# Another order of the projections over the heads of a fused attention and feed-forward kernel, and a constant copy in four parts

## The reference

```python
xn = layernorm(x)
q, k, v = xn @ Wq + bq, xn @ Wk + bk, xn @ Wv + bv          # 16 heads of 32 columns
scores = q @ k.T / sqrt(32) + slope[head] * distance         # causal
attn_out = softmax(scores) @ v @ Wo + bo
gate_w, up_w, down_w = cubic interpolation of control points # 2048 x 512, 2048 x 512, 512 x 2048
ffn_out = (silu(xn @ gate_w.T) * (xn @ up_w.T)) @ down_w.T
out = x + attn_out + ffn_out                                
```

## Time and profile before

| | us |
|---|---|
| median of three runs | 837.47 (837.46 to 837.83) |
| the profiled execution | 838.84 |
| its span from first to last instruction | 837.0 |
| attention, first scores to the start of feed-forward | 37.97 to 524.87 |
| TensorE busy | 711.5 (85%) |
| VectorE busy | 507.2 (61%) |
| ScalarE busy | 439.3 (52%) |
| GpSimd busy | 332.3 (40%) |
| mean granted TensorE clock | 0.922 |

### The profile page before, as it was taken

How to read it: one execution, slowest core, us unless ns; L and a number is a source line. 1 busy time by engine, 2 the same in 40 slices (tenths; PEclk the granted TensorE clock), 3 DMA queues, 4 the chain that set the end, 5 groups by cost and what they waited for, 6 DMA issues and landing times. The chain is left out here.

```text
span 837.0 us, 14001 instructions
## 1 busy us (share of the span) xinstructions
PE 711.5 (85%) x4884; PEld 563.2 (67%) x4884; DVE 507.2 (61%) x1289; ACT 439.3 (52%) x961; POOL 332.3 (40%) x191
## 2 busy tenths in 40 slices
PE   5678779889789888898898676677978999999997
PEld 4556557667677776676676565455766888888886
DVE  6286687798979888967888688556432222222212
ACT  4266576687657766756877672334332333233321
POOL 2343453444534545534544450112214325425434
PEclk9878789899979999898999799679898999999999
DMA  7982654553584346465437945756616646433201
GB/s 254 188 219 37 111 74 155 76 76 65 114 182 101 48 76 114 93 173 77 67 68 210 252 143 170 245 153 187 208 51 196 224 118 202 153 108 105 101 1 50
DMA packets 53023, 109.78 MB, mean 131 GB/s; under 512 B 6361, under 2 KB 6617, under 8 KB 51417
## 3 DMA queue, kind: packets, MB, share of 16 engines
q1 hardware_dynamic: 51368, 106.46, 51.2%
q10 hardware_dynamic: 1584, 2.43, 1.2%
HBM read 59.32 MB, written 25.17 MB: 101 GB/s over the span
## 5 line engine op out<-in xcount | busy, mean ns | idle before, releaser
L1132 POOL TENSOR_TENSOR work<-work 128x1280 f16<-128x1280 f32 x64 | 168.4, 2632 | 235.2 <-DVE work L816 234.9
L1029 ACT ACTIVATE work<-work,neg_max 128x128 f32<-128x128 f32 (+3 forms) x256 | 142.3, 564 | 106.7 <-DVE neg_max L808 105.9
L1581 POOL TENSOR_TENSOR in_lo<-inner,in_hi 128x512 fp32r<-128x512 f32 x64 | 85.3, 1335 | 221.8 <-ACT in_hi L1497 221.8
L808 DVE CUSTOM_DVE_ANT_0 work<-bank,dist 128x128 f32<-128x128 f32 (+3 forms) x256 | 115.3, 487 | 89.0 <-PE bank L600 70.7
L1544 DVE TENSOR_TENSOR inner<-bank,silu 128x512 f32<-128x512 f32 x64 | 44.1, 689 | 136.0 <-ACT silu L1491 125.1
L1038 ACT COPY work<-bank 128x768 f16<-128x768 f16 (+1 forms) x128 | 110.0, 909 | 30.7 <-PE bank L614 29.5
L600 PE MATMUL bank<-k_stack,q_stack 96*128 96x256 f32 (+2 forms) x256 | 81.4, 396 | 45.2 <-issue 25.5
L1497 ACT CAST in_hi<-inner 128x512 fp32r<-128x512 f32 x64 | 39.7, 621 | 151.2 <-PE bank L1441 144.3
L614 PE MATMUL bank<-ident,work 128*128 128x128 f16 x1280 | 109.5, 230 | 10.2 <-DVE work L823 8.0
L614 PEld LDWEIGHTS bank<-ident,work 128*128 128x128 f16 x1280 | 78.4, 104 | 50.8 <-issue 35.2
L1439 PE MATMUL bank<-w_room,in_hi 128*128 128x512 f32 x256 | 102.7, 401 | 0.5 <-POOL in_lo L1581 0.5
(11 more groups left out here) (100 smaller groups left out, 1411.8 us busy)
## 6 DMA issues: line engine op xcount, KB each, us to landing
q_stack<-parts SPq DMA_DIRECT2D x48, 256.0 KB, 5.6
k_stack<-parts SPq DMA_DIRECT2D x48, 256.0 KB, 5.7
z<-xt_scratch SPq DMA_DIRECT2D x128, 88.0 KB
x_in<-x SPq DMA_DIRECT2D x32, 256.0 KB, 5.5
xt_scratch<-xt_room SPq DMA_DIRECT2D x8, 1024.0 KB, 6.8
xt_room<-xt_scratch SPq DMA_DIRECT2D x6, 1024.0 KB, 11.0
factor<-c_basis SPq DMA_DIRECT2D x5, 1024.0 KB, 7.9
taps<-windows SPq DMA_DIRECT2D x5, 1024.0 KB, 9.8
```

Source lines behind the costliest of these rows:

```text
L808: dve.tensor_tensor_reduce(probs[:, s % 2, OFF[i]:OFF[i] + n], score_bank[i % 2][:, 0:n], dist[:, S - n:S], -slope(s), 3.4e38, ALU.add, AL ...
L1029: e = act.activation(tile, tile, ACT.Exp, bias=neg_max[:, s % 2, i:i + 1], scale=-1.0, accum_out=row_sum[:, s % 4, i:i + 1])
L1132: pool.tensor_tensor(probs16[:, s % 2, 1, :], probs[:, s % 2, :], probs16[:, s % 2, 0, :], ALU.subtract).then_inc(lo_ready, 1)
L1581: pool.tensor_tensor(in_lo[k % 2][:, :], inner[:, k % 2, :], in_hi[:, k % 2, :].bitcast(F32), ALU.subtract).then_inc(il_ready, 1)
```

## The change

The order of units over the steps changes. Key tile 2 is projected at step 3 and not 5, key tile 3 at 8 (was 9), key tile 0 of the next batch at 12 (was 13), key tile 1 at 0 (was 1). q 1 moves to step 13 of the batch before, q 2 to step 1, q 3 to 7, q 0 to 11. The output tiles o 0 to o 3 are at steps 2, 4, 5 and 6 (were 2, 3, 6 and 7), v 1 is at step 13 (was 11). Steps 11 and 13 have two units, 9 and 10 none. Ahead of step 0 of batch 0 come now also v 3 and q 1. On VectorE, o 3 is added in step 7 after the first two maxima. `lay_out` is issued in four parts of 32 rows each between the other DMAs of batch 1's list, and sum 1 is stored behind `stack(b, 2)`.

```diff
--- before.py
+++ after.py
@@ -293,7 +293,7 @@
         in_lo = [room("in_lo0", [P, S], F32R, 78), room("in_lo1", [P, S], F32R, 40)]
 
         def load_basis(sp):
-            sp.wait_ge(bases_st, 16)
+            sp.wait_ge(bases_st, 64)
             sp.dma_start(bm_early[:].bitcast(F32).rearrange("p k e n -> p (k e n)"), moment_d).then_inc(bme_ld, 16)
             sp.dma_start(factor[2][:], c_factor[2]).then_inc(chunk_ld[2], 16)
 
@@ -366,8 +366,11 @@
                     tiles = each[:, m, 4 * (c - 1):4 * c, :].rearrange("p g n -> p (g n)")
                     eng.dma_start(tiles[other].bitcast(F32), tiles[own].bitcast(F32)).then_inc(dup_ld[c], 16)
 
-        def lay_out(sp):
-            sp.dma_start(bases_d, c_bases[:, 0:BM_COLS + BD_COLS]).then_inc(bases_st, 16)
+        def lay_out(sp, part):
+            rows = slice(part * P // 4, (part + 1) * P // 4)
+            sp.dma_start(bases_d[rows], c_bases[rows, 0:BM_COLS + BD_COLS]).then_inc(bases_st, 16)
+            if part:
+                return
             pad = xt_d[:, D:XT_ROWS, :].rearrange("a r n -> a (r n)").rearrange("a (k n) -> a k n", k=P // (2 * B))
             sp.dma_start(pad, c_zero.rearrange("(a k) n -> a k n", a=2 * B)).then_inc(pad_st, 16)
 
@@ -383,9 +386,9 @@
 
 HALF = H // 2
 
-UNITS = {0: [("q", 1)], 1: [("k", 1)], 2: [("o", 0)], 3: [("o", 1)], 4: [("q", 2)], 5: [("k", 2)], 6: [("o", 2)],
-         7: [("o", 3)], 8: [("q", 3)], 9: [("k", 3)], 11: [("v", 0), ("v", 1)], 12: [("q", 0)],
-         13: [("k", 0)], 14: [("v", 2)], 15: [("v", 3)]}
+UNITS = {0: [("k", 1)], 1: [("q", 2)], 2: [("o", 0)], 3: [("k", 2)], 4: [("o", 1)], 5: [("o", 2)], 6: [("o", 3)],
+         7: [("q", 3)], 8: [("k", 3)], 11: [("v", 0), ("q", 0)], 12: [("k", 0)], 13: [("v", 1), ("q", 1)],
+         14: [("v", 2)], 15: [("v", 3)]}
 TURNS = {2: [("c", 3)], 7: [("c", 0)], 9: [("x", 0), ("x", 1)], 10: [("x", 2), ("x", 3)], 11: [("c", 1)],
          15: [("c", 2)]}
 
@@ -404,7 +407,7 @@
     kind, n = key
     if s < HALF:
         return -1 if kind == "o" or key == ("c", 3) else 0
-    return 1 if kind in "xv" or (kind in "qk" and n == 0) else 0
+    return 1 if kind in "xv" or (kind in "qk" and n < 2) else 0
 
 
 def steps_keys(steps, before=True):
@@ -415,8 +418,8 @@
 STACK = 16 * ROLES
 
 
-PJ_FIRST = [("x", t) for t in range(QT)] + [("q", 0), ("k", 0), ("v", 0), ("v", 1), ("v", 2), ("q", 1), ("v", 3),
-                                            ("k", 1)] + steps_keys(range(2, HALF), before=False)
+PJ_FIRST = [("x", t) for t in range(QT)] + [("q", 0), ("k", 0)] + [("v", t) for t in range(QT)] + [("q", 1)] + (
+    steps_keys(range(HALF), before=False))
 PJ_BODY = steps_keys([*range(HALF, H), *range(HALF)])
 
 PJ_BODY_ENDS = list(PJ_BODY)
@@ -424,10 +427,10 @@
 PJ_BODY_ENDS.insert(PJ_BODY_ENDS.index(("c", 3)) + 1, ("o", 0))
 
 MOMENTS = {12: 0, 13: 1, 14: 2}
-PJ_LAST = [("q", 3), ("k", 3), ("c", 1), ("m", 0), ("m", 1), ("m", 2), ("c", 2), ("o", 0), ("o", 1), ("c", 3), ("o", 2), ("o", 3)]
-PJ_LAST_ENDS = [("q", 3), ("k", 3), ("c", 1), ("m", 0), ("m", 1), ("m", 2), ("c", 2), ("c", 3)] + [("o", t) for t in range(QT)]
-
-CARRIED = [("q", 3), ("k", 3)] + [("c", c) for c in range(1, KC)] + [("o", t) for t in range(QT)] + [
+PJ_LAST = [("k", 3), ("c", 1), ("m", 0), ("m", 1), ("m", 2), ("c", 2), ("o", 0), ("o", 1), ("c", 3), ("o", 2), ("o", 3)]
+PJ_LAST_ENDS = [("k", 3), ("c", 1), ("m", 0), ("m", 1), ("m", 2), ("c", 2), ("c", 3)] + [("o", t) for t in range(QT)]
+
+CARRIED = [("k", 3)] + [("c", c) for c in range(1, KC)] + [("o", t) for t in range(QT)] + [
     ("m", m) for m in range(3)]
 
 
@@ -724,12 +727,11 @@
                 turn_x(0, t)
             project_qk(0, "q", 0)
             project_qk(0, "k", 0)
-            for t in range(3):
+            for t in range(QT):
                 project_v(0, t)
+            project_qk(0, "q", 1)
             for s in range(HALF):
                 step(0, s, False)
-                if s == 0:
-                    project_v(0, 3)
             for b in range(1, B):
                 for s in range(HALF, H):
                     step(b - 1, s, True)
@@ -871,8 +873,6 @@
                         v_take(of, n)
                     elif kind == "o" and n > 0:
                         add_residual(of, n)
-                if not later(b) and s in (0, 1):
-                    v_take(b, s + 2)
                 if halved:
                     probs_high(*halved)
                 if s < H:
@@ -898,8 +898,6 @@
                     (x_low if kind == "x" else ctx_low)(of, n)
                 if carry and s == 3:
                     add_residual(b - 1, 0)
-                if carry and s == HALF - 1:
-                    add_residual(b - 1, QT - 1)
                 if carry and s in (8, 9):
                     norm_stats(b + 1, (2 * s - 16, 2 * s - 15))
                 for half, t in SPLITS.get(s, []):
@@ -943,7 +941,7 @@
             dve.tensor_tensor(parts[:, 1, :], qk_full[:], parts[:, 0, :].bitcast(F32), ALU.subtract
                               ).then_inc(ql_ready, 1)
             dve.wait_ge(dist_ld, 16)
-            for t in range(2):
+            for t in range(QT):
                 v_take(0, t)
             dve.wait_ge(wl_pool, 4)
             dve.wait_ge(wl_ready, 4)
@@ -1092,6 +1090,7 @@
             w_high(7)
             for t in range(2):
                 v_high(0, 0, t)
+            qk_high(0, "q", 1)
             for s in range(HALF):
                 step(0, s, False)
             for b in range(1, B):
@@ -1156,6 +1155,7 @@
                 pool.wait_ge(wh_ready, n + 1)
                 pool.tensor_tensor(w_piece(w_lo, n), w_raw[:, n % 3], w_piece(w_hi, n).bitcast(F32),
                                    ALU.subtract).then_inc(wl_pool, 1)
+            qk_low(0, "q", 1)
             for s in range(HALF):
                 step(0, s, False, False)
             for b in range(1, B):
@@ -1224,26 +1224,31 @@
                 load_piece(n)
             stack(0, 0)
             store_xt(0)
-
-            lay_out(sp)
             stack(0, 1)
             stack(0, 2)
             for b in range(1, B):
                 for t in range(QT):
                     load_x(b, t)
                 stack(b - 1, 3)
+                if b == 1:
+                    lay_out(sp, 0)
                 for q in range(QT):
                     sp.wait_ge(pj_full, pj_total(("x", q), b))
                     sp.nop(nofuse=True)
                     load_residual(b - 1, q)
                 store_xt(b)
                 stack(b, 0)
+                if b == 1:
+                    lay_out(sp, 1)
                 stack(b, 1)
+                if b == 1:
+                    lay_out(sp, 2)
                 store_sum(b - 1, 0)
-                store_sum(b - 1, 1)
                 stack(b, 2)
-                store_sum(b - 1, 2)
-                store_sum(b - 1, 3)
+                if b == 1:
+                    lay_out(sp, 3)
+                for q in range(1, QT):
+                    store_sum(b - 1, q)
                 for q in range(QT):
                     sp.wait_ge(res_st[q], 16 * b)
                 sp.nop(nofuse=True)
```

## The result

The changed kernel takes 800.84 us, median of 4 runs (796.64 to 803.49), against 837.47; the ratio is 0.9558, 95% interval 0.9511 to 0.9606. The forecast was 812, so the sign was right and the gain, 36.6 us, was 10.6 us larger than the 26.0 forecast; the time lies 1.2 us under the range.

A forecast was written before the change was run, and what follows sets the result against it. Attention was taken as TensorE-bound except for waits before scores, low-clock steps after them, and VectorE-bound steps 9 and 10. 14.3 + 10.4 + 8.4 + 3.4 - 10.5 = 26.0 us off 837.47 gave 812, range 802 to 823.

The forecast's parts named there:

- The six waits: TensorE's waits before scores at steps 0 and 8 of batches 1 to 3 go whole: 14.3 us less.
- The clock: Four steps (8 or 0) at the lower clock after a wait return to the upper one: 10.4 us less.
- The start: Steps 0 to 7 of batch 0 take 49.5 us, 8.4 less; v3 and q1 ahead of step 0 are hidden.
- The last batch: Step 12 of batch 3 comes 5.6 us earlier, 3.4 of it not yet counted; part of its wait stays.
- so k3 is bound by the queue: Last batch: q3 and k3 copies lie in the DMA queue behind residual loads, moment constants and the 1 MB factor.
- What it adds: Costs in steps 8 to 11 and 13 of batches 0 to 2: 3.5 us a batch, 10.5 in all.
- The +1.0 for q3's L1127 in step 8: POOL's low part of q3 meets VectorE's L839, which bounds through step 10: 1.0 us more a batch.
- The wait for x_low in step 11: Second unit there, q0, needs all x columns and waits for x_low: 0.6 us more a batch.
- rival (b): Clock falls earlier in step 9, stays low through 11, about 3 us a batch: 817 to 825, chance 0.18.
- Rival (c): Another engine, VectorE in steps 5 to 7 or ACT, takes over once waits go: 823 us, chance 0.12.
- Rival (d): Batch 0 reaches VectorE's bound of 44 and the end's queue has room, 10 us more gained: 802, chance 0.09.
- Rival (e): Idle time before L600 is the sequencer's own at these code places, so waits stay: 844 us, chance 0.03.

The follow-up runs named there:

- k0_early: Kernel before with q0 and k0 one step earlier each (11 and 12) and v1 two steps later (13): 828.28 us, ratio 0.9881.
- lay_whole: Changed kernel with the constants copied in one piece at their old place, behind the first store of xt: 805.60 us, ratio 0.9636.
- v3_late: Changed kernel with v3 and its v_take back behind the scores of step 0 of batch 0: 805.73 us, ratio 0.9604.
- q1_at_0: Changed kernel with q1 back beside k1 in step 0 of every batch and one unit in step 13: 819.61 us, ratio 0.9803.
- k2_early: Kernel before with q2 at step 3, k2 at 4, o1 at 5, and sum 1 stored behind the c = 2 stacks: 824.55 us, ratio 0.9849.
- k3_at_9: Changed kernel with q3 back in step 8, k3 in step 9, and no unit in step 7: 811.84 us, ratio 0.9693.
- low_first: Kernel before with a key's low part (L1127) ahead of probs_low (L1132) on POOL: 836.50 us, ratio 0.9986.

## Why the prediction was right in sign and too small

The six waits: the mechanism was right, and all nine but one went. **The step that failed is the price: "So the six at steps 0 and 8 of batches 1 to 3 go whole: 25.5 - 2.94 - 2.89 - 5.41 = 14.3 us".** They measured 18.4. I took the idle rows for the cost of the waits. Each wait cost 0.7 us more than its row in the mean, and step 15 before and in k0_early shows of what: 0.24 in how the record's end is modelled, and 0.5 because the late key's L1127 met VectorE's L793 (1.50 instead of 0.41 us). I had costed that kind of meeting in steps 8 and 10, and not in the steps 7 and 15 that these waits end.

The clock: 10.3 for 10.4, shown by the step windows, and by k0_early alone for steps 0 (5.61 us in all three batches, where two had taken 8.5).

The start: -10.5 for -8.4, with 1.1 given back by a later start. Step 4 began 25.5 us after step 0 (I had 25.8). Steps 4 to 7 took 21.90 where I had 22.19 + 1.4, since VectorE itself was busy for less there (21.10, from 22.19), and POOL too (11.77, from 13.01). The 1.1 us is in the load ahead of attention, where the kernels here scatter: step 0 began at 38.1 in lay_whole, 38.3 in v3_late and 39.4 in q1_at_0, and at 39.7 in k2_early, which has the start of the kernel before (37.97). What I called free, v3 ahead of step 0, is indeed worth having (v3_late, 2.4 us or more). But the forecast took the four parts of the constants for neutral and did not see what they cover: without them 3.6 us come back through ACT's room `parts`.

The last batch: -3.8 for -3.4, but then 1.5 more behind step 12, 0.9 of it in step 12 itself. A wait of 2.41 us is left where I said some 4. Here the number was luck, and the step "so k3 is bound by the queue" failed: k3_at_9 has o3 at step 6 and its load of factor 2 4.8 us earlier, and still takes 26.1 us to step 12, as before (25.9). What gained the time is k3's own step, worth 4.0 us: its first copy leaves 11.5 us into step 8 and not 17.1, but the copies take up to 9.2 us to land instead of 7.4, so of 5.6 us 3.8 are left.

**What it adds is the other step that failed: "Together 3.5 us, three times: 10.5".** The table has 8.6 - 1.3 - 1.4 = 5.9. Of its terms, the second unit of step 13 was right to 0.1 us a batch. The +1.0 for q3's L1127 in step 8 came in small part: L841 there took 0.61 to 0.65 us in batches 1 to 3, not 1.35 (1.23 in batch 0), and steps 9 and 10 got 0.4 us a batch shorter. The wait for x_low in step 11 came as forecast (0.7 to 0.8 us), but was outweighed by the clock. Step 9 without its unit does let the clock fall earlier, as rival (b) said, but rival (b) had the sign wrong: the low stretch moves out of step 11, which TensorE bounds, into step 9, where VectorE bounds, and in two batches of three it is over by step 11. It is cheap there, not free: the pair of L769 in step 10 took 0.95 us less in each batch (0.99, not 1.94), and steps 9 and 10 together only 0.4. k3_at_9 shows the move by putting the unit back: step 9 is then at the upper clock and step 11 takes 11.7 us each time. How the clock falls from one execution to the next is not settled; it moves step 3 (9.4 to 11.9 us) and step 11 (9.7 to 11.2), and the spread of 7 us between the runs fits that.

Rival (c), another engine, is seen in part: VectorE is busy for 5.49 of the 5.59 us of step 8, but TensorE has no wait there. Its new waits on VectorE before L603 are in step 9 of batches 0 to 2 (1.9 to 2.5 us each), which VectorE bounds anyway. In k2_early, where step 9 kept its unit, steps 8 to 10 of batch 1 lost 0.9 us. Rival (d) gave about the right time (802), by other means than it said: batch 0 reached 47.4 us and not VectorE's 44. Rival (e) is dead: the waits went with the landings.

So the sum missed 10.1 us: waits 4.1, what it adds 4.6, the start 1.0 net and the last batch 1.9, less 1.4 for low clock in step 3.

## What to carry to other kernels

Price a wait by comparing the whole step with and without it, not by its idle row: a late producer also runs its side work (here POOL's low part) where it gets in another engine's way, and an early one doesn't. When work is moved off an engine, ask in whose step the clock's low stretch lands; in a step that another engine bounds it was nearly free here. And list for each moved unit every single room it passes through (`qk_full`, `parts`): a second q or k unit in step 0 made step 2 of batch 1 2.4 us longer through one such room, and an unrelated 3 MB copy cost 3.6 us through another.

## What was unexpected of the hardware

- Six copies of 256 KB to ranges of 32 partitions, issued 0.6 us apart within each three, landed about 2 us apart: 14.6 us from the first issue to the last landing, and 14.2 when the second three followed 2.7 us closer (low_first).
- The same step 3 takes 9.4 to 11.9 us in the two profiles of the kernel after, by where the lower clock falls (granted 0.82 to 0.71 over the step).
- Two L769 in a row, which have one tensor as input each, take 0.99 us alone and 1.94 beside GpSimd's L1126 (steps 10 and 9 of batch 1 in the kernel after).
